# Who issues the two small DMAs of a quad's maxima: SyncE or ScalarE, in a post-norm transformer block

## The reference, cut to what matters

```
qkv = x @ Wqkv + bqkv;  q, k, v = split into 16 heads of 16
scores = q @ k^T / 4 + slope[h] * (j - i), masked for j > i
x1 = layernorm(x + softmax(scores) @ v @ Wo + bo)
up, gate = x1 @ ternary(W_up)^T, x1 @ ternary(W_gate)^T       # 1024 wide
out = layernorm(x1 + (silu(up) * gate) @ ternary(W_down)^T)
```

## Time and profile before

| | before |
|---|---|
| runs, us | 622.59, 624.9, 625.31; median 624.9 |
| profiled execution, us | 621.73, its span 620.0 |
| PE busy | 582.8 us, 94% of the span |
| DVE busy | 494.3 us, 80% |
| ACT busy | 318.8 us, 51% |
| POOL busy | 299.0 us, 48% |
| share of PE in the chain that ended last | 78% |

### The profile page before, as it was taken

How to read it: one execution, slowest core, us unless ns; L and a number is a source line. 1 busy time by engine, 2 the same in 40 slices (tenths; PEclk the granted TensorE clock), 3 DMA queues, 4 the chain that set the end, 5 groups by cost and what they waited for, 6 DMA issues and landing times.

```text
span 620.0 us, 13168 instructions
## 1 busy us (share of the span) xinstructions
PE 582.8 (94%) x4152; PEld 348.0 (56%) x4152; DVE 494.3 (80%) x1258; ACT 318.8 (51%) x593; POOL 299.0 (48%) x504
## 2 busy tenths in 40 slices
PE   6779888999999999999999999999999999999795
PEld 4344354654656555664656656574566646546474
DVE  5388968996799859988599868989599877993766
ACT  2129713558347645477246644476255753576152
POOL 1306695346265535465175534564264543554234
PEclk9799999999999999999999999999999999999989
DMA  6865715015451073603553073502554053600001
GB/s 173 278 171 206 212 44 167 23 52 158 128 159 52 3 238 110 161 1 107 164 158 80 1 217 114 174 3 75 163 161 110 1 183 89 205 1 4 34 1 35
DMA packets 47724, 68.49 MB, mean 110 GB/s; under 512 B 4857, under 2 KB 43641, under 8 KB 44793
## 3 DMA queue, kind: packets, MB, share of 16 engines
q1 hardware_dynamic: 47691, 68.08, 37.2%
HBM read 38.44 MB, written 29.36 MB: 109 GB/s over the span
## 4 chain that ended last, share of the span: by engine, by line
PE 78%; DVE 6%; ACT 5%; POOL 5%; issue 3%; DMA 2%; SPq 1%; POOLq 0%; DVEq 0%
PE ring L690 18%; PE max_bank L613 10%; PE acc L643 9%; PE ring L631 9%; PE acc L707 7%; PE ring L589 7%; PE ring L596 4%; ACT probs L764 4%; PE ring L667 4%; PE max_bank L616 2%; PE ring L651 2%; POOL probs L1034 2%; POOL tern_down L1077 1%; PE ring L676 1%; PE ring L579 1%
## 5 line engine op out<-in xcount | busy, mean ns | idle before, releaser
L764 ACT ACTIVATE probs<-ring 128x512 f32<-128x512 f32 x320 | 170.7, 606 | 46.0 <-PE ring L631 44.3
L1034 POOL TENSOR_SCALAR_AFFINE_SELECT probs<-probs 128x256 f32<-128x256 f32 (+1 forms) x320 | 120.5, 402 | 131.8 <-ACT probs L764 131.1
L888 DVE CUSTOM_DVE_ANT_0 max_bank<-max_bank,causal_wide 128x384 f32<-128x384 f32 (+1 forms) x256 | 157.1, 636 | 15.7 <-PE max_bank L613 13.1
L613 PE MATMUL max_bank<-k_stack,q_stack 112*128 112x384 bf16 (+3 forms) x512 | 131.8, 304 | 6.9 <-DVE neg_max L888 3.1
L1070 POOL TENSOR_TENSOR hidden_lo<-hidden,hidden_hi 128x512 f16<-128x512 f32 (+1 forms) x72 | 75.2, 1050 | 63.8 <-ACT hidden_hi L795 63.5
L631 PE MATMUL ring<-q_stack,k_stack 114*128 114x512 bf16 (+3 forms) x512 | 103.7, 300 | 1.5 <-DVE attn L913 0.5
L783 ACT ACTIVATE gating<-ring,tanh_scale 128x512 f32<-128x512 f32 (+1 forms) x72 | 45.9, 639 | 74.6 <-PE ring L690 74.5
L643 PE MATMUL acc<-probs,v_ones 128*32 128x512 f32 (+3 forms) x1024 | 79.9, 438 | 2.8 <-POOL probs L1034 2.8
L613 PEld LDWEIGHTS max_bank<-k_stack,q_stack 112*128 112x128 bf16 x512 | 50.0, 98 | 45.2 <-DVE neg_max L888 15.4
L892 DVE TENSOR_REDUCE neg_max<-max_bank 128x2 f32<-128x512 f32 (+1 forms) x96 | 63.7, 685 | 10.7 <-PE max_bank L616 9.1
L631 PEld LDWEIGHTS ring<-q_stack,k_stack 114*128 114x128 bf16 x512 | 43.8, 97 | 48.2 <-issue 17.0
(11 more groups left out here) (105 smaller groups left out, 887.9 us busy)
## 6 DMA issues: line engine op xcount, KB each, us to landing
q_stack<-qk_scratch SPq DMA_DIRECT2D x15, 768.0 KB, 6.0
k_stack<-k_slots SPq DMA_DIRECT2D x15, 768.0 KB, 7.6
qk_scratch<-qk_parts SPq DMA_DIRECT2D x16, 384.0 KB, 3.0
k_slots<-qk_parts SPq DMA_DIRECT2D x16, 384.0 KB, 2.6
xin<-x_dram SPq DMA_DIRECT2D x8, 512.0 KB, 3.6
qk_scratch<-qk_parts SPq DMA_DIRECT2D x16, 256.0 KB, 3.3
k_slots<-qk_parts SPq DMA_DIRECT2D x16, 256.0 KB, 2.3
res<-x_dram SPq DMA_DIRECT2D x8, 512.0 KB, 3.4
```

What stands on the lines that cost most here:

```text
L613: mm = pe.matmul(o, q_stack[0:MAX_ROW, 4 * g + h, P * tile:P * (tile + 1)], k_stack[0:MAX_ROW, 4 * g + h, 0:width], start=True, stop=tile ...
L764: rg.drained(act.activation(probs[:, g % 2, n, :], rg.bank(step)[:, :], ACT.Exp), step)
L888: dve.tensor_tensor_reduce(scores, scores, causal_wide[:, SEQ - width:SEQ], -1.0, LOWEST_START, ALU.add, ALU.min, neg_max[:, g, first_col: ...
L1034: return pool.affine_select(out=v, in_=v, compare_op=ALU.is_ge, fill=0.0, base=0, pattern=([[0, blocks]] if blocks > 1 else []) + [[1, P]] ...
```

## The change

The step `mt_out.g` now has its two DMAs on ScalarE and none on SyncE. On ScalarE they stand where the step stands in the same lists: ScalarE waits until DVE has drained the ring bank, and issues both DMAs before it goes on to the next activation. SyncE no longer waits there. The DMAs themselves, their data, and the semaphore that `exp.g.0` waits for are the same; DVE, PE and POOL have the same instructions in the same order.

```diff
-                    elif kind == "mt_out":
-                        g = step[1]
-                        rg.wait_drained(sp, ("mt", g))
-                        sp.sem_inc(sp_passed, 1)
-                        for part in range(2):
-                            sp.dma_start(
-                                q_stack[MAX_ROW + part:MAX_ROW + part + 1, 4 * g:4 * g + 4, :],
-                                max_parts[0:4 * TT, g, part, :],
-                            ).then_inc(max_in[g], 16)
...
+                    elif kind == "mt_out":
+                        g = step[1]
+                        rg.wait_drained(act, ("mt", g))
+                        act.sem_inc(act_passed, 1)
+                        for part in range(2):
+                            act.dma_start(
+                                q_stack[MAX_ROW + part:MAX_ROW + part + 1, 4 * g:4 * g + 4, :],
+                                max_parts[0:4 * TT, g, part, :],
+                            ).then_inc(max_in[g], 16)
```

More of the change, by code:

```diff
@@ L327, in block_kernel @@
         bias_folded = sem("bias_folded")
-        dve_passed, pool_passed, sp_passed = sem("dve_passed"), sem("pool_passed"), sem("sp_passed")
+        dve_passed, pool_passed, act_passed, sp_passed = (sem(f"{e}_passed") for e in ("dve", "pool", "act", "sp"))
         consts_set = sem("consts_set")
```

## The result

| | before | after |
|---|---|---|
| runs, us | 622.59, 624.9, 625.31, 627.88 | 666.03, 668.68, 677.23, 678.74 |
| median | 625.11 | 672.95 |
| profiled execution (span) | 621.73 (620.0) | 666.03 (664.3) |
| granted clock, mean | 0.987 | 0.962 |

The change makes the kernel slower by 6.75%: ratio 1.0675, 95% interval 1.059 to 1.076. (A ratio leaves out executions over 1.5% above the fastest of the same kernel, here those of 677 and 679 us, with a granted clock of 0.950 and 0.948, while the medians count all.) The forecast was 641, with 652 as its upper end: right in sign, much too small. The two profiled executions differ by 44.3 us, and that is what has to be explained.

The account below looks back on a forecast made before the run. TensorE was taken as the bound, with nothing to give. 10.5 + 5.6 + 0.9 + 0.7 - 0.4 = 17.3 us on the profiled 621.7; taking 16.1 on the median of 624.9 gave 641.0 us, range 632 to 652.

Parts of the forecast that it names:

- case 1: DMAs start late behind ScalarE's activation: PE stands 2.1 us in each loop pass, 10.5 us; outside the loop 5.6 us.
- start of the activation ahead, plus 0.56, plus 1.7: Landing time of the second small DMA: ScalarE's preceding activation starts, second issue 0.56 us later, landing 1.7 us after that.
- rival of the dearer issue: ScalarE ends its activation before issuing, or issues more slowly: 20 to 30 us over 624.9, about 649; chance 17%.
- covers of quads 1 to 3: In the loop, ACT's idle pieces and PE's banks ahead absorb the 1.14 us of issuing: 0 us lost.
- Point (5): Profile sign: ACT's idle time in quads 1 to 3 shortened, without PE waits.
- (1) to (3): Signs: some 11 PE waits for max_parts, longest 2.1 us; first issue within 0.1 us of tanh start; issues 0.56, landings 1.7.
- (6): Profile sign: no wait of PE for `xin` at `tx.0` in FIRST.
- (4): Profile sign: a loop pass longer by 2.1 us, with PE busy 36.5 of 38.6 us.
- I use this 2.3 everywhere: Second landing taken as 2.3 us after the preceding activation's start at every place, in the loop and outside.
- `xin` in FIRST: SyncE, freed, starts this load earlier, so PE's 0.41 us wait at `tx.0` goes: -0.4 us.
- SECOND quad 2, ACT blocked: Two exponentials at 134.13 start late with no cover, delaying `pv.0.0`: 0.9 us.
- Case 2: ScalarE held up 1.14 us by two issues: 0 in the loop, 0.9 in SECOND quad 2, 0.7 in FIRST quad 1.

Follow-up runs that it names:

- e3: Kernel before, SyncE issuing, but in the loop its quad 0 DMAs also wait for PE's product of up.7: 638.92 us, ratio 1.0265.
- e7: e1 with ScalarE's quad 0 issue in the loop moved ahead of the tanh of up.6: 625.62 us, ratio 1.0028.
- e8: Changed kernel with SyncE's hold from e5, the earlier quad 0 issue from e7 and GpSimd's wait from e11: 636.92 us, ratio 1.019.
- run 12: Not a run label: the text says the changed kernel's whole run had 12 waits where 11 were forecast; its profiled execution took 666.03 us.
- e5: Changed kernel, but SyncE waits at its old place until ScalarE's two small DMAs have landed: 658.75 us, ratio 1.0533.
- e4: Changed kernel with 7 to 20 discarded matmuls on PE ahead of the first score matmul of six quads: 656.05 us, ratio 1.0543.
- e11: e6 with GpSimd also waiting for DVE's two ternary passes ahead of its own: 632.69 us, ratio 1.0134.
- e6: Kernel before, SyncE issuing; ScalarE waits for the same drain and issues two same-size DMAs to unused rows: 635.98 us, ratio 1.0113.
- e9: Kernel before, SyncE issuing, but in the loop its quad 0 DMAs also wait for PE's product of up.6: 629.04 us, ratio 1.0091.
- e1: Kernel before with ScalarE issuing the two DMAs only in the loop's five passes, SyncE elsewhere: 641.51 us, ratio 1.0303.
- e2: Kernel before with ScalarE issuing in the twelve places outside the loop, SyncE in the loop: 653.01 us, ratio 1.0507.
- e10: Changed kernel, with GpSimd's first pass over the down weights waiting for both of DVE's ternary passes: 667.11 us, ratio 1.0725.

## Why the prediction was wrong in size, and right in sign and in one of three causes

**Right: the bound and case 1 in the loop.** PE had nothing to give, and the lateness of ACT's order became PE's stand: 2.22 us a pass against the 2.1 forecast, 11.1 against 10.5. Each element of "start of the activation ahead, plus 0.56, plus 1.7" held (0.09, 0.56, 1.80). The rival of the dearer issue is refuted by the same rows: ACT issues while its activation runs. e3 showed that it is the place and not the engine, e7 that moving the place mends it for the loop.

**Right: the covers of quads 1 to 3.** Seen in the timeline; e8 prices it at 0.04 us in five passes. Point (5) of what to look for held, and so did (1) to (3) for the loop (in the whole run 12 waits for 11, the longest 4.6 and not 2.1), and (6). (4) missed: passes were longer by 2.4, and three of them by 4.0.

**Failed: "I use this 2.3 everywhere".** The 1.7 in it was measured where no large transfer stood ahead, and was not what the small DMAs met where one did. Outside the loop the waits summed to 17.7, not 5.6: FIRST quad 0 3.6 (forecast 0), SECOND quad 3 4.3 (0.7), SEVENTH quad 0 4.6 (0.7), FIRST quad 3 2.5 (1.4). Three others stood (SECOND quad 0 1.9 against 1.8, SEVENTH quads 1 and 2 0.4 and 0.5 against 0.2 and 0.8). With the transfers held back in e5 the sum was 6.0. So the arithmetic was right for the world that it assumed. The sentence at fault stands ahead of it: "64 issues leave SyncE, whose time nobody pays for". Its time nobody paid for, but its *waiting* was an order: nothing behind `mt_out` could start before the small DMAs had gone. I saw this for FIRST, priced it at 0 to 2 us and left it out of the sum; it was 3.6. For the stack reads of SECOND and SEVENTH I didn't look at what stood behind L546 in the queue, though 148.31 and 533.67 were there to be read. I expected the small ones to share with the loads and not to stand behind all of them, and took that to be cheap. Only FIRST bears out the sharing, where they landed ahead of four loads issued before them. In SECOND they landed 0.05 and 0.31 us after the stack read ahead of them: they stood behind all of it.

**Failed: no term for the clock.** The sum took PE's stand as the whole of the loss. Behind three of the loop's five stands of 2.2 us the clock was halved for 3.4 us, and PE's matmuls then took some 1.64 us more. Over the program PE is busy 15.0 us longer. Some 2 of them belong to the start, so at most 13 are the clock behind the stands. e4 left 1.1 of the 15.0 while each pass stayed 2.3 longer. The row for it before the change was the clock column: 0.987 on the mean, with a drop of 3.4 us still at 590.0, behind a stand of 3.1 us at the last batch's `x1t.0`. It should have been asked of each new stand.

**Small terms.** `xin` in FIRST: its wait is gone, as forecast. SECOND quad 2, ACT blocked: 1.5 against 0.9. Case 2 was too cheap in SECOND and probably in SEVENTH (e11: 0.8 us there, forecast 0).

The sum, mended on the profiled execution: 11.1 + 6.0 (late starts) + 11.7 (overtaking transfers) + 15.0 (longer busy time, of it at most 13 the clock behind the stands) = 43.8 of 44.3. The forecast had 16.1 for the first two terms, which measured 17.1, and nothing for the other two. The start of the program isn't explained: at FIRST quad 0 the lag was between -0.7 and 5.2 us in the profiled executions without a wait for `max_parts` there, and in the changed kernel 1.7 us of it were there before the first small DMA.

## What to carry to other kernels

An engine that sits waiting in front of an issue is also a gate for everything behind it in its queue. Before work is taken off such a queue, list what stands behind it, when that will start instead, and which small, urgent transfer it will meet. A moved issue inherits the place of the instruction ahead of it, and a stand of PE is to be priced with the clock that follows it: here 2.2 us of waiting cost up to 4.0.

## What the runs showed of the hardware

- DVE's two ternary passes over 128x2048 took 1.31 and 2.37 us with GpSimd's pass begun after the second had begun, and 5.3 and 5.7 with it begun before both; GpSimd's took 7.47 in the one case and 5.45 in the other. An order of start that nothing fixed was worth 9 us of PE's time (e5, e6).
- A 4 KB DMA (0.27 MB in 64) landed 1.7 us after its issue on quiet DMA engines, and 5.1 to 6.2 us with loads of 512 or 768 KB under way on the other queue, at a DMA share of 0.75 to 1.05. In SECOND it landed within 0.1 to 0.3 us of the read issued 2.5 us ahead of it on the other queue; in e7, beside one `xin` load, it landed in 2.8 to 3.1.
- PE stands of 1.0 us were followed by half a clock in none of five passes (e9), of 2.0 to 2.3 us in three to five of five (the changed kernel, e1, e3, e5). Length alone doesn't decide: the stand of 1.9 us at SECOND quad 0 was followed by none in any of the five kernels that have it (the changed one, e2, e5, e8, e10), and the same program ahead of the loop has a half-clock stretch near 100 us in e3, e7 and e9 and none in the kernel before.
